# A macaron layer in float32: how its fp8 weights are rounded, in how many pieces, and on which engines, on one core

## The reference, cut to what matters

```python
def quantized_matmul(x, w, scale):
    wq = w.astype(float8_e4m3fn).astype(x.dtype)
    return (x @ wq) * scale

def ffn(x):                        # H = 256, I = 768
    gate = silu(quantized_matmul(x, gate_w, gate_scale))
    up = quantized_matmul(x, up_w, up_scale)
    return quantized_matmul(gate * up, down_w, down_scale)

x = x + 0.5 * ffn(layernorm(x))
x = x + attn(layernorm(x))         # 16 heads, rotation, decay mask, group norm, silu gate
x = x + 0.5 * ffn(layernorm(x))
```

## Time and profile before

| | us |
|---|---|
| median of 3 runs | 178.29 (178.2 to 178.42) |
| the profiled execution, its own time | 178.39 |
| its span in the profile | 176.6 |
| TensorE busy | 163.6 (93% of the span) |
| VectorE busy | 137.0 (78%) |
| ScalarE busy | 75.6 (43%) |
| GpSimd busy | 67.6 (38%) |

### The profile page before, as it was taken

How to read it: one execution, slowest core, us unless ns; L and a number is a source line. 1 busy time by engine, 2 the same in 40 slices (tenths; PEclk the granted TensorE clock), 3 DMA queues, 4 the chain that set the end, 5 groups by cost and what they waited for, 6 DMA issues and landing times.

```text
span 176.6 us, 3264 instructions
## 1 busy us (share of the span) xinstructions
PE 163.6 (93%) x1125; PEld 124.8 (71%) x1125; DVE 137.0 (78%) x294; ACT 75.6 (43%) x162; POOL 67.6 (38%) x76
## 2 busy tenths in 40 slices
PE   5997989899899999998999999999889899799992
PEld 2355756688779776866686868777658688798881
DVE  2899899999834395778696969979778797765763
ACT  3153498767205024233434160614616546225510
POOL 3445293453844311334462827463495420000000
PEclk9999999999999999999999999999999999999999
DMA  5898105403000000000000000000000000011002
GB/s 158 282 347 295 64 2 175 181 4 121 0 4 0 0 0 4 0 0 4 2 0 4 2 0 0 4 0 6 0 0 2 0 4 0 0 59 59 6 30 89
DMA packets 6848, 8.41 MB, mean 48 GB/s; under 512 B 416, under 2 KB 5552, under 8 KB 6832
## 3 DMA queue, kind: packets, MB, share of 16 engines
q1 hardware_dynamic: 6832, 8.20, 13.7%
HBM read 7.15 MB, written 1.05 MB: 46 GB/s over the span
## 4 chain that ended last, share of the span: by engine, by line
PE 59%; DVE 23%; issue 6%; ACT 5%; POOL 3%; DMA 2%; SPq 0%; DVEq 0%; ACTq 0%
PE bank L991 15%; PE bank L1019 9%; PE bank L1112 8%; PE bank L1047 6%; DVE fuse L660 3%; PE bank L1168 3%; DVE sc L715 3%; PE bank L1058 3%; PE bank L1061 3%; PE bank L1090 2%; PE bank L1106 2%; DVE grid L574 2%; DVE h L632 2%; DMA xt<-in_L_attn_x 2%; PE bank L1073 2%
## 5 line engine op out<-in xcount | busy, mean ns | idle before, releaser
L991 PE MATMUL bank<-hh,gate_r 128*128 128x512 f32 x96 | 27.9, 408 | 3.6 <-DVE hh L644 2.1
L991 PE MATMUL bank<-hh,up_r 128*128 128x512 f32 x96 | 26.3, 396 | 0.0
L1019 PE MATMUL bank<-down_r,fhi 128*128 128x256 f32 x96 | 24.3, 291 | 0.3 <-DVE flo L668 0.3
L324 POOL TENSOR_TENSOR grstd<-gve,neg_half 128x16 f32<-128x16 f32 x8 | 23.3, 2907 | 0.7
L1019 PE MATMUL bank<-down_r,flo 128*128 128x256 f32 x96 | 23.4, 282 | 0.0
L991 PEld LDWEIGHTS bank<-hh,gate_r 128*128 128x128 f32 x96 | 16.7, 188 | 9.5 <-issue 3.8
L408 ACT ACTIVATE gact<-bank,vec 128x512 f32<-128x512 f32 x24 | 16.5, 686 | 16.0 <-PE bank L991 15.7
L660 DVE SCALAR_TENSOR_TENSOR fuse<-bank,vec,gact 128x512 f32<-128x512 f32 x24 | 17.9, 746 | 5.3 <-PE bank L991 5.1
L991 PEld LDWEIGHTS bank<-hh,up_r 128*128 128x128 f32 x96 | 18.1, 188 | 4.2
L715 DVE TENSOR_TENSOR sc<-bank,msk 128x512 f32<-128x512 f32 x32 | 20.3, 682 | 0.0
L1019 PEld LDWEIGHTS bank<-down_r,fhi 128*128 128x128 f32 x96 | 18.1, 188 | 1.2 <-DVE flo L668 0.6
(11 more groups left out here) (80 smaller groups left out, 301.0 us busy)
## 6 DMA issues: line engine op xcount, KB each, us to landing
raw<-in_rotation SPq DMA_DIRECT2D x1, 1536.0 KB, 6.5
xt<-in_L_attn_x SPq DMA_DIRECT2D x2, 512.0 KB, 4.6
out<-xt SPq DMA_DIRECT2D x8, 128.0 KB, 1.7
raw<-in_L_ffn_down_w SPq DMA_DIRECT2D x2, 384.0 KB, 7.6
wqkv<-in_L_attn_w_qkv SPq DMA_DIRECT2D x1, 768.0 KB, 9.4
raw<-in_rotation SPq DMA_DIRECT2D x1, 512.0 KB, 3.3
raw<-in_L_ffn_gate_w SPq DMA_DIRECT2D x1, 384.0 KB, 6.1
raw<-in_L_ffn_up_w SPq DMA_DIRECT2D x1, 384.0 KB, 6.7
```

The lines of the kernel that those rows point to most:

```text
L324: pool.tensor_tensor(grstd[:, c % 2], gve[:, :], neg_half[:, :], ALU.pow).then_inc(grstd_done, 1)
L991: mm = pe.matmul(dst[:, :], wr[m][:, k * I + i * P:k * I + (i + 1) * P], half[:, k, g % NG, :], start=(k == 0 and half is hhi), stop=(k == ...
L1019: mm = pe.matmul(downs[d][:, 0:C], half[:, g % NG, i, t * P:(t + 1) * P], wr["down"][:, i * C:(i + 1) * C], start=(i == 0 and half is fhi) ...
```

## The change

- A piece is first lifted on ScalarE: `lift` copies the raw piece into `grid` times 2^20, and VectorE's three passes are `grid_step` in place, `grid_add` (maximum with the smallest step and add, in one `scalar_tensor_tensor`, into `raw`) and `grid_sub` (the same maximum, minus the sum, back into `grid`). `grid_clip` is gone, no subtract is on GpSimd, and `to_weights` reads `grid` directly, with the sign and the scale; `to_half` and `w16` are gone. `grid` has four slots. The scales of h, fuse and the vectors are changed to fit; `rest_h` becomes a `scalar_tensor_tensor`.
- Ten pieces: the cuts are 0, 128, 384, 512, 768.
- `PRODUCTS` takes blocks 0 to 2 of both groups, then block 3 of both, then blocks 4 and 5 of group 0 and of group 1.
- The tiles 0, 2, 4 and 6 of h are normalised on ScalarE (`norm_act`), with a vector `shift` from VectorE (`shift_rows`); the others stay on VectorE.
- The first four tiles of x come as two loads; piece 3 is loaded before the masks.
- `gate_up(0)` is `first_gate_up`: both high parts, then both rests. `turn_h(1)` stands behind `gate_up(2)` and not behind `gate_up(0)`. Seven products with zeros stand between the rest, before it were nine.
- The lists of VectorE, ScalarE and GpSimd are rearranged.

```diff
-GRID = 2.0 ** -20
-GRID_MIN = 1.5 * 2.0 ** -6
-W_SCALE = 144.0
-CUTS = [0, 128, 384, 768]
+LIFT = 2.0 ** 20
+GRID_MIN = 1.5 * 2.0 ** -6 * LIFT
+W_SCALE = 1.125 * 2.0 ** 119
+H_SCALE = 2.0 ** -90
+F_SCALE = 2.0 ** -60
+GRID_SLOTS = 4
+
+CUTS = [0, 128, 384, 512, 768]
...
 PIECES = [(m, a, b) for a, b in zip(CUTS, CUTS[1:]) for m in ("gate", "up")] + [("down", 0, 3), ("down", 3, 6)]
-SUB_ON_POOL = [0, 1, 2, 3, 4, 6]
...
-PRODUCTS = ([(g, i) for g in range(NG) for i in range(3)] + [(g, i) for g in range(NG) for i in range(3, NI)]
+PRODUCTS = ([(g, i) for g in range(NG) for i in range(3)] + [(g, 3) for g in range(NG)]
+            + [(g, i) for g in range(NG) for i in range(4, NI)]
             + [(g, i) for g in range(NG, 2 * NG) for i in range(NI)])
-PIECES_NEEDED = [2, 4, 4, 6, 6, 6]
+PIECES_NEEDED = [2, 4, 4, 6, 8, 8]
...
             load_piece(0)
-            sp.dma_start(xt[:, 0:TH, :], x_dram[0]).then_inc(x_in[0], 16)
+            sp.dma_start(xt[:, 0:2, :], x_dram[0][:, 0:2, :]).then_inc(x_in[0], 16)
+            sp.dma_start(xt[:, 2:TH, :], x_dram[0][:, 2:TH, :]).then_inc(x_in[1], 16)
             load_piece(1)
             load_piece(2)
+            load_piece(3)
             sp.dma_start(msk[:, :], mask_t).then_inc(mask_in, 16)
             for src, at, n in ((gate_s, 0, NI), (up_s, NI, NI), (gn_w, 2 * NI, KC), (gn_b, 2 * NI + KC, KC)):
                 sp.dma_start(rows[at:at + n, :], src.rearrange("(i p) -> i p", p=P)).then_inc(rows_in, 16)
-            sp.dma_start(xt[:, TH:NT, :], x_dram[1]).then_inc(x_in[1], 16)
-            for q in range(3, len(PIECES)):
+            sp.dma_start(xt[:, TH:NT, :], x_dram[1]).then_inc(x_in[2], 16)
...
             pool.wait_ge(const_done, 1)
-            subtract(0)
             roots(0)
-            for n in range(1, 4):
-                subtract(n)
             roots(1)
-            subtract(4)
             for n in range(0, 3):
                 rest_f(n)
-            subtract(6)
             rest_f(6)
             rest_f(8)
             add_down(0)
...
         def _(act):
-            def to_half(q):
-
-                if q in SUB_ON_POOL:
-                    act.wait_ge(sub_pool, subs(q + 1)[1])
-                else:
-                    act.wait_ge(sub_dve, subs(q + 1)[0])
-                if q >= 2:
-                    act.wait_ge(w_ready, q - 1)
-                nc.scalar.activation(packed(w16, q), packed(grid, q), ACT.Copy,
-                                     scale=W_SCALE / GRID).then_inc(half_done, 1)
+            def lift(q):
+
+                act.wait_ge(raw_in[q], 16)
+                if q >= GRID_SLOTS:
+                    act.wait_ge(w_ready, q - GRID_SLOTS + 1)
+                nc.scalar.activation(packed(grid, q), piece(raws[PIECES[q][0]], q), ACT.Copy,
+                                     scale=LIFT).then_inc(lifted, 1)
 
             def to_weights(q):
 
-                act.wait_ge(half_done, q + 1)
-                nc.scalar.activation(piece(wr[PIECES[q][0]][:, :], q), packed(w16, q), ACT.Copy).then_inc(w_ready, 1)
+                act.wait_ge(sub_done, q + 1)
+                nc.scalar.activation(piece(wr[PIECES[q][0]][:, :], q), packed(grid, q), ACT.Copy,
+                                     scale=-W_SCALE).then_inc(w_ready, 1)
+
+            def norm_act(n):
+
+                act.wait_ge(shift_done, n // TH + 1)
+                if n >= TH:
+                    act.wait_ge(turned, n - TH + 1)
+                nc.scalar.activation(h[:, n % TH, :], xt[:, n, :], ACT.Identity, scale=rstd[:, n:n + 1],
+                                     bias=shift[:, n:n + 1]).then_inc(h_act, 1)
 
...
 
-                dve.wait_ge(raw_in[q], 16)
-                if q >= 2:
-                    dve.wait_ge(half_done, q - 1)
-                dve.tensor_scalar(packed(grid, q).bitcast(U32), piece(raws[PIECES[q][0]], q).bitcast(U32),
+                dve.wait_ge(lifted, q + 1)
+                dve.tensor_scalar(packed(grid, q).bitcast(U32), packed(grid, q).bitcast(U32),
                                   EXP_BITS, HALF_BIT, ALU.bitwise_and, ALU.bitwise_or).then_inc(exp_done, 1)
 
-            def grid_clip(q):
+            def grid_add(q):
 
                 dve.wait_ge(exp_done, q + 1)
-                dve.tensor_scalar(packed(grid, q), packed(grid, q), GRID_MIN, None, ALU.max).then_inc(clip_done, 1)
-
-            def grid_add(q):
-
-                dve.wait_ge(clip_done, q + 1)
                 w = piece(raws[PIECES[q][0]], q)
-                dve.scalar_tensor_tensor(out=w, in0=w, scalar=GRID, in1=packed(grid, q),
-                                         op0=ALU.mult, op1=ALU.add).then_inc(added, 1)
-
-            def subtract(q):
+                dve.scalar_tensor_tensor(out=w, in0=packed(grid, q), scalar=GRID_MIN, in1=w,
+                                         op0=ALU.max, op1=ALU.add).then_inc(added, 1)
+
+            def grid_sub(q):
 
                 dve.wait_ge(added, q + 1)
-                dve.tensor_tensor(packed(grid, q), piece(raws[PIECES[q][0]], q), packed(grid, q),
-                                  ALU.subtract).then_inc(sub_dve, 1)
+                dve.scalar_tensor_tensor(out=packed(grid, q), in0=packed(grid, q), scalar=GRID_MIN,
+                                         in1=piece(raws[PIECES[q][0]], q),
+                                         op0=ALU.max, op1=ALU.subtract).then_inc(sub_done, 1)
+
+            def shift_rows(g):
+
+                a, b = root_groups[g]
+                dve.wait_ge(rstd_done, g + 1)
+                dve.scalar_tensor_tensor(out=shift[:, a:b], in0=mv[:, a:b, 0], scalar=-1.0, in1=rstd[:, a:b],
+                                         op0=ALU.mult, op1=ALU.mult).then_inc(shift_done, 1)
 
...
                 for t in range(TH):
-                    if g == 0 and t == 1:
-                        keep_busy(1)
-                    pe.wait_ge(h_done, n0 + t + 1)
+                    if g < NG and t % 2 == 0:
+                        pe.wait_ge(h_act, g * TH // 2 + t // 2 + 1)
+                    else:
+                        pe.wait_ge(h_done, normed_until(n0 + t))
                     for k in range(KC):
                         mm = pe.transpose(turn[g][k][:, t * P:(t + 1) * P], h[:, (n0 + t) % TH, k * P:(k + 1) * P], ident)
                     mm.then_inc(turned, 1)
+
+            def first_gate_up():
+
+                pe.wait_ge(hhi_done, KC)
+                for half in (hhi, hlo):
+                    if half is hlo:
+                        pe.wait_ge(hlo_done, KC)
+                    for m in ("gate", "up"):
+                        pe.wait_ge(w_ready, 1 if m == "gate" else PIECES_NEEDED[0])
+                        for k in range(KC):
+                            mm = pe.matmul(pairs[0][0][m == "up"][:, :], wr[m][:, k * I:k * I + P], half[:, k, 0, :],
+                                           start=(k == 0 and half is hhi), stop=(k == KC - 1 and half is hlo))
+                        if half is hlo:
+                            mm.then_inc(gate_done if m == "gate" else up_done, 1)
 
...
                         if half is hlo:
-                            if j == 0 and m == "gate":
-                                keep_busy(4)
...
             pe.transpose(bank[7][:, 0:2 * NI + 2 * KC], rows[:, :], ident[0:2 * NI + 2 * KC, 0:2 * NI + 2 * KC]).then_inc(vec_turned, 1)
-            keep_busy(2)
             turn_h(0)
-            keep_busy(2)
-            gate_up(0)
+            keep_busy(1)
+            first_gate_up()
+            keep_busy(4)
+            gate_up(1)
+            gate_up(2)
+            keep_busy(1)
             turn_h(1)
-            for j in range(1, 9):
+            keep_busy(1)
+            for j in range(3, 9):
```

170 lines of the change are left out of this document (90 added, 80 removed).

## The result

| | before | changed |
|---|---|---|
| median | 178.35 us (4 runs) | 183.97 us (4 runs, 182.4 to 184.32) |
| ratio, 95% interval | | 1.0299 [1.0252, 1.0347] |
| profiled execution, its span | 178.39, 176.6 | 184.32, 182.5 |
| VectorE, GpSimd busy | 137.0, 67.6 | 135.9, 58.7 |

Slower, as forecast; 183.97 is 2.3 us above the number and 0.17 us above the range. The same kernel, measured once more (experiment 11), gave 182.71, so that its ten runs fall into two places: six from 182.4 to 182.72, four from 183.89 to 184.36. What stands between them is TensorE's clock: its mean over the span was 0.991 in each of the four and 1.00 in each of the six.

The account below looks back on a forecast made before the run. TensorE, with VectorE nearly full, was taken to bound the first feed-forward block. The second half of `down(0)` at 45.1 instead of 41.7 adds 3.4 us to 178.39, less 0.1 for the median: 181.7 us, range 179.3 to 183.8.

Parts of the forecast that it names:

- The place: First feed-forward block: when TensorE begins the second half of `down(0)` (41.72 before) moves the end; under 1 us of room behind.
- The wait by the order of products: Before the second half of `down(0)`: product (0, 5) comes one later, TensorE waits 2.4 us for `rest_f(9)`, at least 1.6.
- `down(0)` waits for it 1.9 us: First `down`: TensorE waits 1.9 us, to 37.54, for ScalarE's `to_weights(8)` behind the blocked `grid_sub(8)`.
- The early lead: TensorE starts `gate_up(3)` at 21.46 against 23.31, 1.85 us ahead; the lead is gone after the waits before `gate_up(4)` and `(5)`.
- rival 2: Faster: VectorE's passes between two fuses fit TensorE's 1.86 us a product, the lead stays; -1.25 us, 177.0 us; chance 0.12.
- The exclusion: VectorE passes and GpSimd's `rest_f` lock each other out of SBUF ports: blocked 1.10, 0.40, 0.40, 0.41 and 0.96 us.
- the walk: The new queues laid out instruction by instruction with durations from the trace; on the old queues it gave 41.43 for 41.72.
- Without any lock ... about no change: If VectorE and GpSimd did not block each other in the new kernel, the sum would come out at about no change.
- The sum: Second half of `down(0)` at 45.1 less 41.7 gives +3.4 us, so 181.7 us.
- Rival 3: TensorE's longer waits bring the half clock for some 3 us of products: 3 us more, 184.7; chance 0.08.
- h tiles on ScalarE: Four h tiles of 0.32 us leave VectorE for ScalarE, 0.57 us each there (bounds 0.46 and 0.67).
- VectorE's waits: In the first block VectorE waits 0.65, 0.97, 1.12 and 0.55 us, together 3.3, as much as the subtracts gave back.

Follow-up runs that it names:

- experiment 11: The changed kernel as it is, measured once more: 182.71 us, five runs at 182.52 to 182.72 and one at 184.36.
- experiment 3: The kernel before with the new order of products alone: 179.77 us, 1.0092.
- experiment 6: The changed kernel with VectorE's and ScalarE's lists rearranged, its own new order of products kept and `rest_f(9)` ahead of `scale_down(0)`: 177.69 us, 0.9954.
- experiment 2: The changed kernel with four products of zeros on TensorE in its wait before the second half of `down(0)`: 182.33 us, 1.0225.
- experiment 1: The changed kernel with the old order of products, all else as changed: 180.6 us, 1.0135.
- experiment 5: The changed kernel with the old order of products and VectorE's and ScalarE's lists of the first block rearranged: 176.03 us, 0.9861.
- experiment 8: The changed kernel with the old order of products, GpSimd's rests of `fuse` replaced by memsets that read nothing: 177.25 us, 0.9943.
- experiment 9: The changed kernel with the old order of products, all eight h tiles normalised on VectorE and no shift: 180.96 us, 1.015.
- experiment 4: The changed kernel with the old order of products and only VectorE's list of the first block rearranged: 179.63 us over ten runs, 1.0064.
- experiment 7: The kernel before, its own instructions, with VectorE's and ScalarE's lists of the first block rearranged: 176.32 us, 0.9902.
- experiment 10: The changed kernel with three products of zeros before the first half of `down(0)`, none before the second: 182.62 us, two of six runs near 184.

## Why the prediction was right, and where not

- **The place.** Right: what the second half of `down(0)` is late, the end is late. At the full clock (experiment 11) it starts 45.93-41.72 = 4.2 us later, and the span is 180.7-176.6 = 4.1 us longer.
- **The wait by the order of products.** Right in place, releaser and size: 2.4 us forecast, 2.28 measured; its minimum was forecast as 1.6 and measured as 1.63 and 1.66 (experiments 3 and 6). Taken out, it is worth 1.4 to 1.7 us in three pairs of kernels at the full clock (2 and 1, 3 and the kernel before, 6 and 5).
- **"`down(0)` waits for it 1.9 us".** 1.69 us, for ScalarE's `down_r`, behind a pass that was blocked for 0.44 us (0.41 forecast). The waits before `gate_up(4)` and `(5)` were 1.31 and 0.77 for 1.5 and 1.0. The early lead went there, so rival 2 was rightly small.
- **The exclusion.** Right: five passes were blocked for 3.4 us, where the walk had 3.3 (1.10, 0.40, 0.40, 0.41 and 0.96). It costs 2.2 us at the second half of `down(0)` (experiment 8, with the old order of products). "Without any lock ... about no change" was worked out with the new order. With all that experiment 8 gained that is 177.25+1.7 = 179.0, 0.8 us above the kernel before; with the 2.2 us alone it is 182.71-2.2 = 180.5, 1.8 above the 178.72 beside it. Both are estimates, since the two were not run together.
- **The sum.** 45.1 was forecast, 45.93 measured at the full clock. Part of it lies in the walk: `gate_up(1)` at 15.45 for 15.27, and from there to `gate_up(3)` 6.51 us for 6.19. In the profiled run of 184.32 us `gate_up(1)` came at 15.79, as TensorE had waited 1.39 us for the `rows` loads, which now stand behind one more piece and have no term in the sum. And the walk ran 0.3 us early on the kernel before; I said so, and then subtracted the traced 41.72 instead of the walked 41.43. With like against like, 45.1-41.43 = 3.7 gives 182.0, and 4.0 was measured at the full clock (182.71 against 178.72 beside it).
- **Rival 3, the clock.** This is the step that failed. "The clock falls" was given 0.08 and laid out as another outcome of the kernel. It is an outcome of single runs, four of ten, and comes on top of the forecast: 182.4 to 182.7 us without it, 183.9 to 184.4 with it. That three of the first four runs had it, and so their median, is luck as far as the runs show: in experiment 11 it was one of six. The trace of the kernel before shows no half clock, so the "3 us of products" had no row behind them. It costs 1.7 us and not 3: the clock was 0.51 for 3.5 us of time, and at half speed that is 1.7 us of products. The waits were listed there, one of 2.4 us where none had been over 1.03, and they should have moved both its chance and the upper end of the range.
- **h tiles on ScalarE.** 0.55 us a tile (two in 1.09) for 0.57, and worth nothing that could be measured (experiment 9).
- **What I took as given.** VectorE's waits, 3.3 us in the walk and 0.47+1.35+1.18+0.68 = 3.68 in the trace. With the lists rearranged the same work ran 180.6-176.03 = 4.6 us faster (experiments 1 and 5).

So the loss at the full clock, 4.0 us, is 1.7 by the order of products and 2.3 by the rest (180.6 against 178.34): passes in whole chains between fuses, that meet GpSimd's rests there. Experiments 5 and 8 each remove more than that rest, one by order and one by what GpSimd reads; their gains were not measured together and are no sum.

## What to carry to other kernels

Before work moves between engines to relieve one, look at what that engine waits for: VectorE had 3.7 us of waits in its list, and what the h tiles on ScalarE gave went into them. Rearranging two lists was worth about 2 us in the kernel before and 4.6 in the changed one. When the order of products changes, follow each consumer that counts them: one block one place later cost 1.4 to 1.7 us three times. Where TensorE waits for over 2 us, products with zeros in the wait can be tried: four of them cost nothing that was measured (182.33 us), and the clock stayed in all four runs, which is too few to call it a remedy. And when the runs of one kernel spread over more than 1 us, compare each run's mean clock before anything else; here it sorted them in experiments 4, 5, 7, 10 and 11.

## What was new about the hardware

- Behind a wait of 2.28 us, TensorE's granted clock was 0.51 for 3.5 us in one profile and 1.00 in another of the same program, with its waits of 1.7 and 2.28 us alike; four of ten times are 1.7 us higher. Behind waits of 1.63 to 1.71 us it stayed at 1.00 in the profiles here, and in all 19 runs of experiments 1, 3, 6 and 9 its mean was 0.996 or more. The Trainium skill ("TensorE: Matmul & The Clock Gate", "Part 1") has the clock halved behind idleness; the trace agrees, in some of the runs.
- In experiment 4 the clock was 0.51 from 14.00 to 17.50 us, with no wait over 0.8 us since TensorE's first product at 1.77; TensorE was busy for 2.48 of the 4 us before.
- A memset on GpSimd leaves a two-input pass of VectorE that starts beside it at its size (0.43 us), where a subtraction on GpSimd made the same pass 1.53. In the other direction the memset keeps its 0.53 us behind a running pass of VectorE, where the subtraction took 1.87 for 1.33.
- A `tensor_scalar` of VectorE isn't quite free beside a memset: the h tile at 46.79 in experiment 8 takes 0.57 us for 0.40, with a memset of GpSimd from 46.69 to 47.22. That is one instance.
